# A macaron block with a selective scan: down product and output projection with tokens on the partitions, the residual kept, decays made two states at a time

## The reference, cut to what matters

```python
x = x + 0.5 * ffn(layernorm(x))          # 8 experts of 176, top 2 by a router, and a shared one of 352
x = x + attn(layernorm(x))               # the state-space layer below
x = x + 0.5 * ffn(layernorm(x))

# ffn:  y = sum_e w[t, e] * (silu(x W1[e]) * (x W2[e])) W3[e]  +  (silu(x Ws1) * (x Ws2)) Ws3
# attn, on r = layernorm(x):
xz = r @ W_in + b_in ; x_in, z = split(xz)
xc = silu(conv4(x_in) + conv_b)                          # 256 inner channels
B, C = split(xc @ W_xp + b_xp)                           # 16 states
delta = softplus(xc @ W_dt + b_dt)
h[t] = exp(delta[t] * A) * h[t-1] + delta[t] * xc[t] * B[t]     # per channel and state
y = (sum_s h * C + D_skip * xc) * silu(z)
attn = layernorm_unbiased(r + y @ W_out + b_out, alpha, beta)
```

## Time and profile before

| | |
|---|---|
| median of three runs | 2232.82 us (2228.62 to 2250.01) |
| the profiled execution | 2241.29 us, span 2239.5 us |
| mean granted TensorE clock | 0.887 |
| busy share PE / DVE / ACT / POOL | 80% / 73% / 69% / 64% |
| chain that ended last, by engine | PE 43%, ACT 21%, DVE 17%, "issue" 12%, POOL 3% |
| scan of group 2 starts / scan of group 14 starts | 358.6 / 1942.5 us |

### The profile page before, as it was taken

How to read it: one execution, slowest core, us unless ns; L and a number is a source line. 1 busy time by engine, 2 the same in 40 slices (tenths; PEclk the granted TensorE clock), 3 DMA queues, 4 the chain that set the end, 5 groups by cost and what they waited for, 6 DMA issues and landing times.

```text
span 2239.5 us, 22836 instructions
## 1 busy us (share of the span) xinstructions
PE 1794.9 (80%) x4674; PEld 804.4 (36%) x4674; DVE 1639.6 (73%) x2505; ACT 1535.3 (69%) x2083; POOL 1441.3 (64%) x1286
## 2 busy tenths in 40 slices
PE   3878587979888888887888798788888878885577
PEld 1433233434334333333433343333333433332233
DVE  2257878687786878878687877878778786879742
ACT  1257587777778767786876778687677867776522
POOL 3346676666667675776767666676766676676753
PEclk9989788989898898998989898898989889897698
DMA  4117565555556555555555654655556555557642
GB/s 130 45 55 178 119 164 130 144 133 143 127 142 153 130 135 134 152 132 151 152 137 129 152 143 127 151 147 140 130 131 159 131 145 138 133 122 173 150 111 61
DMA packets 119129, 300.05 MB, mean 134 GB/s; under 512 B 19184, under 2 KB 40400, under 8 KB 104656
## 3 DMA queue, kind: packets, MB, share of 16 engines
q0 software_dynamic: 18432, 125.84, 28.1%
q1 hardware_dynamic: 92672, 168.88, 24.2%
q10 hardware_dynamic: 7888, 4.09, 0.7%
HBM read 167.67 MB, written 5.24 MB: 77 GB/s over the span
## 4 chain that ended last, share of the span: by engine, by line
PE 43%; ACT 21%; DVE 17%; issue 12%; POOL 3%; ACTq 1%; DMA 1%; DVEq 0%; POOLq 0%
PE ps_y L1043 9%; PE ps_h2a L1048 6%; DVE hist L868 5%; PE ps_m L1003 5%; ACT L680 5%; PE ps_h1a L1030 4%; PE ps_h1b L1030 4%; ACT L657 4%; PE ps_h2b L1048 4%; DVE den L912 3%; ACT decay L657 3%; ACT silu L680 2%; DVE yacc L950 2%; PE ps_m L1110 2%; DVE ps_db L834 2%
## 5 line engine op out<-in xcount | busy, mean ns | idle before, releaser
L569 POOL TENSOR_TENSOR prod<-hist,crow 128x1024 f32<-128x1024 f32 x224 | 556.0, 2482 | 371.8 <-DVE hist L868 368.0
L1043 PE MATMUL ps_y<-gated,down_w 128*128 128x512 f32 (+1 forms) x896 | 517.6, 664 | 101.3 <-POOL gated L521 63.2
L868 DVE TENSOR_TENSOR_SCAN hist<-decay,ps_db 128x1024 f32<-128x1024 f32 x256 | 583.2, 2278 | 13.8 <-issue 11.3
L521 POOL TENSOR_TENSOR gated<-gated,silu 128x512 f32<-128x512 f32 x352 | 476.3, 1416 | 138.1 <-DVE gated L860 108.4
L834 DVE TENSOR_TENSOR ps_db<-du,ps_db 128x1024 f32<-128x1024 f32 x256 | 313.7, 1225 | 319.1 <-PE ps_db L1012 318.8
L657 ACT ACTIVATE decay<-delta,a_neg 128x510 f32<-128x510 f32 x512 | 338.1, 711 | 2.6
L1048 PE MATMUL ps_h2a<-xnT,up_w 128*128 128x512 f32 (+1 forms) x448 | 253.2, 649 | 53.3 <-DVE gated L860 53.3
L680 ACT ACT_TABLE_LOAD x227 | 291.2, 1283 | 5.5 <-issue 0.7
L1043 PEld LDWEIGHTS ps_y<-gated,down_w 128*128 128x128 f32 (+1 forms) x896 | 180.3, 209 | 319.3 <-issue 218.0
L1030 PE MATMUL ps_h1a<-xnT,up_w 128*128 128x512 f32 (+1 forms) x448 | 248.0, 636 | 49.7 <-ACT silu L680 48.8
L657 ACT ACT_TABLE_LOAD x217 | 278.4, 1283 | 3.8
(11 more groups left out here) (137 smaller groups left out, 2242.5 us busy)
## 6 DMA issues: line engine op xcount, KB each, us to landing
yacc<-prod POOLq DMA_DIRECT2D x112, 1024.0 KB, 9.0
crow<-c_rows SPq DMA_DIRECT2D x128, 512.0 KB, 4.2
wrow<-w_rows SPq DMA_DIRECT2D x320, 128.0 KB, 3.6
wrow<-w_rows SPq DMA_DIRECT2D x64, 224.0 KB, 3.2
wrow<-w_rows SPq DMA_DIRECT2D x64, 192.0 KB, 3.6
wrow<-w_rows SPq DMA_DIRECT2D x64, 160.0 KB, 3.4
yacc<-yacc POOLq DMA_DIRECT2D x16, 512.0 KB, 6.2
wrow<-w_rows SPq DMA_DIRECT2D x64, 96.0 KB, 3.3
```

What stands on the lines that cost most here:

```text
L521: nc.gpsimd.tensor_tensor(gated[:, pos % NGATE, :], gated[:, pos % NGATE, :], silu[:, (pos + NCHUNK * f_parity(k, f)) % NSILU, :], ALU.mul ...
L569: nc.gpsimd.tensor_tensor(prod[:, (pair - 1 + odd) % 2, s % 2, :, :], hist[:, s % 2, :, :], c_all, ALU.mult).then_inc(prod_done, 1)
L868: nc.vector.tensor_tensor_scan(hist[:, s % 2, :, :].rearrange("p h t -> p (h t)"), decay[:, s % NA, :, :, :].rearrange("p h b t -> p (h b ...
L1043: nc.tensor.matmul(ps_y[:], down_w[0:rd, jd, :], gated[0:rd, posd % NGATE, :], start=(posd == 0), stop=(posd == NCHUNK - 1)).then_inc(down ...
```

## The change

The down product has its operands exchanged: four tiles of 128 tokens of `gated` are stationary and `down_w` moves with 128 columns, so `ps_y` is [token, channel] and `addy` reads it directly. The steps `y0`, `y1`, `yT0` and `yT1` are gone. The output projection is exchanged likewise, its bias comes from a product of a row of ones with a bias row, and `outT` and the copy `oT` are gone. The normalised input is kept in one of two buffers `x1n`, and a DMA in SP's slot 17 (`keep_x1n`) copies it to `rtok`; the step `x1n` on ACT is gone. The decays are made for two states in slots 0, 4, 8 to 24 in place of one state in slots 0, 2, 4 to 26. The steps stand in other slots.

```diff
     PLAN = {
-        0: ["stats0", "y0"], 1: ["yT0", "x1n"], 2: ["addy0", "norm0"], 3: ["stats2", "fold"], 4: ["xT0"],
...
+        0: ["stats0", "addy0"], 1: ["stats2"], 2: ["norm0"], 3: ["norm2", "fold"], 4: ["xT0"], 5: ["logits0"],
...
     SP_PLAN = {
...
+        17: ["keep_x1n"], 18: ["w0:4"], 19: ["c6", "w0:5"], 20: ["w0:6"], 21: ["store_x", "w0:7"], 22: ["w0:8"],
...
-    DECAYS = {2 * s - 4: s for s in range(2, NS)}
+    DECAYS = {4 * i: (2 * i + 2, 2 * i + 3) for i in range(NS // 2 - 1)}
...
+                        elif step == "keep_x1n" and scans(k):
+                            sp.wait_ge(norm_ready[2], k + 1)
+                            if tail(k):
+                                sp.wait_ge(mamba_added, k)
+                            sp.dma_start(rtok[:], x1n[odd][:]).then_inc(x1n_ready, 16)
...
-                        elif step == "x1n" and tail(k):
-
-                            plain_wait()
-                            act.wait_ge(nbias_ready[2], k)
-                            if not isinstance(k, int) or k > 1:
-                                act.wait_ge(mamba_added, k - 1)
-                            normalise(rtok, xres[:, behind, :, :], nbias1[:, nxt, :], rstd1[:, nxt, :]
-                                      ).then_inc(x1n_ready, 1)
...
-                        elif step == "y0" and lead(k) or step == "y1" and last(k):
-                            f = int(step[1])
-                            act.wait_ge(down_done, fcount(k if f else k - 1, f, NCHUNK, NCHUNK))
-                            nc.scalar.activation(yT[:], ps_y[:], ACT.Copy).then_inc(y_taken, 1)
-                        elif step == "outproj" and tail(k):
-                            take(k, step)
-                            nc.scalar.activation(oT[:], ps_m[:], ACT.Identity,
-                                                 bias=b_out_c[:, 0:1]).then_inc(misc_taken, 1)
...
                     elif slot in DECAYS and scans(k):
-                        decays(k, odd, [DECAYS[slot]])
+                        decays(k, odd, DECAYS[slot])
...
                         elif step == "addy0" and lead(k) or step == "addy1" and last(k):
                             f = int(step[4])
-                            dve.wait_ge(misc_full, turn(k, f"yT{f}"))
+                            dve.wait_ge(down_done, fcount(k if f else k - 1, f, NCHUNK, NCHUNK))
                             xr = xres[:, oldest if f else ahead, :, :].rearrange("p t c -> p (t c)")
-                            nc.vector.scalar_tensor_tensor(xr, ps_m[:], 0.5, xr, ALU.mult, ALU.add
-                                                           ).then_inc(misc_taken, 1)
+                            nc.vector.scalar_tensor_tensor(xr, ps_y[:], 0.5, xr, ALU.mult, ALU.add
+                                                           ).then_inc(y_taken, 1)
...
-                        nc.tensor.matmul(ps_y[:], down_w[0:rd, jd, :], gated[0:rd, posd % NGATE, :], start=(posd == 0),
-                                         stop=(posd == NCHUNK - 1)).then_inc(down_done, 1)
+                        for t in range(TILES):
+                            ins = nc.tensor.matmul(ps_y[:, t * C:(t + 1) * C],
+                                                   gated[0:rd, posd % NGATE, t * P:(t + 1) * P], down_w[0:rd, jd, :],
+                                                   start=(posd == 0 and t == 0),
+                                                   stop=(posd == NCHUNK - 1 and t == TILES - 1))
+                        ins.then_inc(down_done, 1)
...
-                            for half in range(HALVES):
-                                ins = nc.tensor.matmul(ps_m[:], w_out[:, half, :], yacc[nxt][:, 0, half, :],
-                                                       start=(half == 0), stop=(half == HALVES - 1))
+                            nc.tensor.matmul(ps_m[:].rearrange("p (t c) -> p t c", t=TILES), ones_r[:],
+                                             b_out_r[:].unsqueeze(1).to_broadcast([1, TILES, C]), start=True,
+                                             stop=False)
+                            for t in range(TILES):
+                                for half in range(HALVES):
+                                    ins = nc.tensor.matmul(ps_m[:, t * C:(t + 1) * C],
+                                                           yacc[nxt][:, 0, half, t * P:(t + 1) * P],
+                                                           w_out[:, half, :], start=False,
+                                                           stop=(t == TILES - 1 and half == HALVES - 1))
```

More of the change, by code:

```diff
@@ L65, in macaron_kernel @@
         0: ["c1"], 3: ["c2"], 4: ["w1:4"], 5: ["w1:5"], 6: ["w1:6"], 7: ["c3", "w1:7"], 8: ["w1:8"], 9: ["w1:9"],
[3 rows of a table removed]
[3 rows of a table added]
     }
-    DECAYS = {2 * s - 4: s for s in range(2, NS)}
+    DECAYS = {4 * i: (2 * i + 2, 2 * i + 3) for i in range(NS // 2 - 1)}
     MISC_ENTRY = ["xT0", "logits0", "wT0"]
-    MISC_LEAD = ["yT0", "xT2", "in0", "in1", "in2", "in3", "dt0", "dt1", "xproj", "cT", "bT"]
-    MISC_TAIL = ["outproj", "outT", "xT1", "logits1", "wT1"]
-    MISC_LAST = ["yT1"]
+    MISC_LEAD = ["xT2", "in0", "in1", "in2", "in3", "dt0", "dt1", "xproj", "cT", "bT"]
+    MISC_TAIL = ["outproj", "xT1", "logits1", "wT1"]
     FULL = 2
@@ L95, in misc_list @@
     def misc_list(k):
[L96 removed]
+        names = (enters(k) * MISC_ENTRY) + (lead(k) * MISC_LEAD) + (tail(k) * MISC_TAIL)
         return [n for s in range(SLOTS) for n in PLAN.get(s, []) if n in names]
@@ L240, in macaron_kernel @@
         stdr = sb("stdr", [P, 3, TILES])
-        xn = [sb(f"xn{f}", [P, TILES, C]) for f in range(2)]
-        xn = [xn[0], xn[0], xn[1]]
+        xn = sb("xn", [P, TILES, C])
+        x1n = [sb(f"x1n{i}", [P, TILES, C]) for i in range(2)]
         xnT = [sb(f"xnT{f}", [P, TG]) for f in range(3)]
@@ L963, in body @@
                             plain_wait()
-                            dve.wait_ge(misc_taken, turn(k, "outT"))
+                            dve.wait_ge(misc_taken, turn(k, "outproj"))
                             statistics(rtok, 3, mvr, stats_no(k, 3))
```

41 lines of the change are left out of this document (18 added, 23 removed), and 14 rows, old and new, of tables (PLAN, SP_PLAN).

## The result

The changed kernel takes 2385.89 us (median of 4 runs, 2381.15 to 2394.66), the kernel before in the same session 2234.21. The ratio is 1.0671, 95% interval 1.0609 to 1.0734: 6.7% slower, where 3.7% faster was forecast.

A forecast was written before the change was run, and what follows sets the result against it. No engine is full; different engines and their hand-overs end the stretches. Terms sum to -6 us per iteration, times 14 is -84; from 2241.3 that gives 2157, less 8.5 for the median: 2150 us (-3.7%), 8-in-10 range 2105 to 2215.

The forecast's parts named there:

- Table loads: Decay batches among the SiLUs fall from 15 to 8, saving 14 loads of 1.283 us, 18.0 us of ACT per iteration.
- Slots 0 to 5, -1.5: Scans 0 to 3, ended by ACT: its work falls from 20.89 to 17.2 us; 1.5 us per iteration gained after friction.
- Slots 6 and 7, 0: Scan 3 to 4: DVE's work stays the same, `gate_y` moves one slot within it, so no change.
- Slots 8 to 15, +1.0: Scans 4 to 8, PE bound: 128-column passes at 0.117 us each make the stretch 1.0 us longer per iteration.
- Slots 16 to 23, -2: Scans 8 to 12: 2 us gained per iteration; at least a loss of 1.4 if DVE replaces the copy.
- the yT argument: Slot 18: PE's 3.2 us wait for copy `yT` goes, since `addy1` on DVE frees `ps_y` one slot ahead.
- Slots 24 to 31, -3.5: Scan 12 to the next iteration: `weights1` moves from slot 28 to 25; 26 us for 29.45, 3.5 gained.
- The hold: DVE held at `den` until GpSimd pauses, perhaps 5.51 us again in slot 25; about 6.4 with three smaller operations.
- 4.5 for 9.84: Scan 14 to 15: 4.5 us instead of 9.84, with DVE at 3.3 and PE about 3 at full clock.
- 5.5 for 6.92: Scan 15 to the next iteration: 5.5 us instead of 6.92, as PE comes from work and not a wait.
- 0.11 for slower: Chance of a slowdown, nearly all from weight load and stream in turn (chance 0.10): 0.224 us per pass, 2325 to 2480 us.
- signs of being wrong: Pass pitch above 0.144 us, a new PE wait for DVE in slot 18, or an iteration above 130 us.

The follow-up runs named there:

- Repaired: The changed kernel with `ln_norm` in slot 15, `gate_y` in slot 6 and `resid` in slot 9: 2217.17 us, ratio 0.9914 to the kernel before.

## Why the prediction was wrong, point by point

The forecast's terms sum to -6 us per iteration; the measured stretches give +1.0, +2.4, +5.0, +2.1 and -0.4, together +10.2. The step that failed is the same in most terms: a moved step was priced by its own work, and not by what it now stands in front of or beside in each engine's queue.

- **What bounds the kernel.** Right: no engine is full, and hand-overs set the pace. It was not carried through: once waits set the pace, each moved step needs its place in every queue looked up, and this was done in full only for SP's.
- **Table loads.** Count and size right (ACT -309 us). Their worth: 12 us in the old schedule, minus 14 to minus 36 in the new one. A pair keeps a SiLU waiting 1.2 us longer than a single decay, and at the start of an iteration PE and DVE are seen waiting for that SiLU; elsewhere the cause stays open.
- **Slots 0 to 5, -1.5.** Repaired and without slot 0's burst it is about -1 (19.2 for 20.2). As made it was +1.0. One part is the burst: "with its work crowded into slots 0 and 1" named DVE's crowd, and missed that ACT's pair lay ahead of the first SiLU of the pipeline. The other is the stall at the loop's return: repaired, the stretch takes 19.4 us in iterations without a return, where it was 21.1 before, about the gain forecast, and 21.4 in those with one, where it was 19.2.
- **Slots 6 and 7, 0.** Failed at "`gate_y` moves by one slot within it": same work, other neighbours. +2.4 us, with two GpSimd gates beside a DVE operation with two SBUF inputs. The prediction had this very mechanism in hand for `den` and didn't ask it of the step that moved.
- **Slots 8 to 15, +1.0.** The price of the passes is right: repaired, the stretch is 34.6 for 34.2. As made it is +5.0. Missed: `resid` behind scan 5 now frees `ps_m`, since `oT` that freed it is gone; and the projection runs at the lower clock.
- **Slots 16 to 23, -2.** The forecast allowed for DVE in place of the copy and took that as at most a 1.4 us loss; the row reads `DVE xres <- PE ps_y`, longest 7.5. It failed one step further back: `ln_norm` moved past a product and a gate in GpSimd's queue, and the gate is what the last down product needs. This is the dearest single miss, 72 us. Repaired, the stretch gives -3.2, which fits the yT argument; no run takes that wait alone.
- **Slots 24 to 31, -3.5.** The move of `weights1` has the wrong sign: slot 28 is 11 to 16 us better than 25. The hold followed it as said, and its size (5.2 to 6.0 for 6.4) was right by luck: `den` takes 0.4 to 1.25 us there and not 5.51, and the operations behind it take the rest. What failed is "4.5 for 9.84" and "5.5 for 6.92": they are 6.8 and 7.55 in iteration 7 of the repaired kernel, as the row of B waits behind products for GpSimd's gates, 3.3 us that the hold had covered, and PE does not come to full clock.
- **Length of the program.** Not in the sum at all. 2720 more matmuls bring a stall of PE at the returns of the loop, 15.9 us of waits in the changed kernel and 18.6 repaired. From scan 12 to scan 3 of the next iteration the repaired kernel takes 50.7 us with a return and 44.9 without, 48.4 and 47.6 before: 5.0 us more per return, some 25 us in all by that estimate.
- **SP and DMA, nothing.** Right: the table of waits has no wait for the copy that `keep_x1n` makes.
- **Rivals and chances.** 0.11 for slower was held for the price of the pass, and that was refuted; the result came by none of the named ways. Of the signs of being wrong one came, an iteration above 130 us; the pitch stayed below 0.144, and the table of waits has no wait of PE for DVE with `addy1`. The rival that was missing is "a moved step stands in front of a gate on GpSimd", and it could have been read from the order of POOL's instructions before the run: `ln_norm` ahead of `prod` and `gated` in slot 14, with an input that ACT makes only behind `in3`.

## What to carry to other kernels

When operations are exchanged and a plan of steps is moved in one change, price the operations by their rows and the moves by queues: for each moved step, on each engine that it issues on, list what it now stands ahead of, when its input is ready, and who waits for what is behind it. Here the exchanged operations with a fitting order and single decays gave 2.7%, and three misplaced steps, each one slot from a better place, cost 7.6%. No run has the exchanged operations in the old order, so how much of the 2.7% is theirs isn't shown. Removing work from an engine that doesn't end the stretches brings little, and grouping it can cost, if the group is longer than the slack of the engine that waits behind it.
